# The feed-forward's first two steps begun on half the images, its steps then taken in threes

## The reference, cut to what matters

```python
x = x + conv_attention(group_norm(x))          # 4 heads of 32
t = tokens(x)                                   # 4 images x 256 tokens x 64
t = t + causal_attention(layer_norm(t))         # 4 heads of 16
xf = layer_norm(t)
gate_logits = xf @ Wg + bg                      # 8 logits a token
top_w, top_i = top_k(gate_logits, 2)
top_w = softmax(top_w)
w_dense = sum(one_hot(top_i, 8) * top_w[..., None], axis=1)
out = 0
for e in range(8):
    h = gelu(xf @ W1[e] + b1[e])                # 64 -> 256, exact gelu
    out = out + w_dense[:, e:e+1] * (h @ W2[e] + b2[e])   # 256 -> 64
t = t + out
```

## Time and profile before

| | us |
|---|---|
| median of 3 runs | 114.43 |
| the profiled execution | 114.85 |
| its span | 112.8 |
| PE busy in the span | 101.8 (90%) |
| DVE busy | 75.4 (67%) |
| ACT busy | 65.1 (58%) |
| granted clock of PE, mean | 0.998 of full |

### The profile page before, as it was taken

The page is one execution under the profiler, slowest core; times in us unless marked ns, Lnnn a source line. Parts: engine busy times, 40 slices in busy tenths (PEclk is TensorE's granted clock), DMA queues, the critical chain, the costliest instruction groups (busy, mean ns, idle before and its releaser), DMA issues.

```text
span 112.8 us, 2251 instructions
## 1 busy us (share of the span) xinstructions
PE 101.8 (90%) x831; PEld 52.8 (47%) x831; DVE 75.4 (67%) x210; ACT 65.1 (58%) x121; POOL 15.8 (14%) x28
## 2 busy tenths in 40 slices
PE   5989978889899999997899998999999999999920
PEld 2346456655555455566666654675342323232300
DVE  6965899979505469999966688998638453155250
ACT  4039973433888756564329958894937644764400
POOL 7900200000000000000000000000003941343140
PEclk9999999999999999999999999999999999999999
DMA  2940000199700000000000000000000000000003
GB/s 74 246 84 7 2 0 9 31 237 189 118 0 0 0 9 0 0 0 0 6 0 6 0 0 0 0 0 3 0 6 0 0 0 0 0 0 0 0 0 93
DMA packets 6633, 3.16 MB, mean 28 GB/s; under 512 B 4432, under 2 KB 6496, under 8 KB 6624
## 3 DMA queue, kind: packets, MB, share of 16 engines
q1 hardware_dynamic: 5936, 2.38, 11.5%
q10 hardware_dynamic: 688, 0.66, 2.3%
HBM read 2.77 MB, written 0.26 MB: 27 GB/s over the span
## 4 chain that ended last, share of the span: by engine, by line
PE 68%; DVE 16%; ACT 10%; issue 3%; DVEq 0%; ACTq 0%
PE bank L933 13%; PE bank L944 13%; PE bank L874 6%; PE bank L807 6%; PE bank L839 5%; PE bank L888 4%; PE bank L858 4%; PE bank L749 3%; PE bank L758 3%; PE bank L721 2%; DVE mx L590 2%; DVE mx L586 2%; ACT sq L399 2%; PE bank L845 1%; ACT sq L405 1%
## 5 line engine op out<-in xcount | busy, mean ns | idle before, releaser
L481 ACT ACTIVATE hid<-bank,b1c 128x1024 f32<-128x1024 f32 x16 | 16.9, 1112 | 11.8 <-PE bank L933 11.8
L437 ACT ACTIVATE pr<-bank 128x1024 f32<-128x1024 f32 (+1 forms) x16 | 14.0, 914 | 8.5 <-PE bank L845 5.1
L933 PE MATMUL bank<-xn,w_sb 64*128 64x512 f32 x64 | 15.6, 612 | 0.0
L944 PE MATMUL bank<-hid,w_sb 128*64 128x512 f32 x64 | 15.3, 603 | 0.0
L705 DVE SCALAR_TENSOR_TENSOR yw<-bank,b2c,wc 128x512 f32<-128x512 f32 x8 | 6.0, 748 | 12.6 <-PE bank L944 12.6
L721 PE MATMUL bank<-still 128*128 128x512 bf16 (+1 forms) x41 | 11.8, 437 | 1.2 <-DVE still L495 1.2
L359 POOL TENSOR_TENSOR acc<-yw,x 64x512 f32<-64x512 f32 x1 | 1.3, 1269 | 72.1 <-DVE yw L705 72.1
L586 DVE TENSOR_REDUCE mx<-bank 128x4 f32<-128x1024 f32 x8 | 9.3, 1218 | 0.9 <-PE bank L807 0.8
L807 PE MATMUL bank<-k,q 32*128 32x256 f32 (+1 forms) x128 | 8.3, 373 | 1.6 <-ACT q L425 0.6
L933 PEld LDWEIGHTS bank<-xn,w_sb 64*128 64x128 f32 x64 | 5.6, 186 | 8.5 <-ACT hid L481 4.4
L364 POOL TENSOR_TENSOR acc<-acc,yw 128x512 f32<-128x512 f32 x6 | 7.6, 1274 | 11.8 <-DVE yw L705 11.6
(11 more groups left out here) (148 smaller groups left out, 176.4 us busy)
## 6 DMA issues: line engine op xcount, KB each, us to landing
w_sb<-in_L_ffn_W_dram SPq DMA_DIRECT2D x3, 512.0 KB, 7.2
x<-in_x_dram ACTq DMA_DIRECT2D x2, 256.0 KB, 4.8
xg<-in_x_dram SPq DMA_DIRECT2D x1, 256.0 KB, 3.2
wg<-in_L_conv_w_qkv_dram SPq DMA_DIRECT2D x2, 96.0 KB, 4.8
bqkv<-in_L_attn_b_qkv_dram SPq DMA_DIRECT2D x12, 0.1 KB, 1.6
wo1t<-in_L_attn_W_out_dram SPq DMA_DIRECT2D x8, 4.0 KB, 1.8
out_dram<-acc SPq DMA_DIRECT2D x1, 128.0 KB, 2.5
out_dram<-acc ACTq DMA_DIRECT2D x1, 128.0 KB, 2.8
```

The lines of the kernel that those rows point to most:

```text
L437: nc.scalar.activation(pr[:, b, 2 * p:2 * p + 2, 0:n], two(key, 0, n), ACT.Exp, scale=SCALE[l]).then_inc(free(key), 1)
L481: nc.scalar.activation(hid[:, k % 4, :, :], two(("h", 0, k)), ACT.Gelu, bias=b1c[:, k:k + 1]).then_inc(free(("h", 0, k)), 1)
L933: i = mm(ps(key, i=s), w1_sb[r, e, P * j:P * j + P], XN[r, 2 * s:2 * s + 2, :].rearrange("p b t -> p (b t)"), start=True, stop=True)
L944: i = mm(ps(key, p0=C * s, p1=C * s + C), w2_sb[:, k, :], hid[:, k % 4, s, :], start=(j == 0), stop=(j == FT - 1))
```

## The change

The first two steps of the feed-forward are split by images. The halves of images 0 and 1 (`uphalf`) stand on PE behind the gate of image 1, ahead of the fillers and the gate of image 2. The halves of images 2 and 3 (`uprest`) stand behind the gate of image 2, ahead of the gate of image 3, which thereby moves behind them. The fillers ahead of the gate of image 3 (4 of 512 columns) go, and 4 of 256 columns stand ahead of `uprest` instead. So that the halves are contiguous per bank, the lower partitions now take images 0 and 2, the upper ones images 1 and 3; the gate tiles, the residual add of POOL and the two stores follow this.

The feed-forward then goes by threes: three ups, three downs. `hid` has 6 buffers for 4. The first such group is up 2, 3, 4, the transposes of the gate weights, up 5, and then downs 0, 1, 2. The bank pairs are 0/1, 4/5, 2/3.

```diff
-    ("gate", 2, (218, 222, 230, 234), ((7,), (2,), (7,), (2,))),
-    ("logits", 2, (221, 231, 233, 235), ()),
+    ("gate", 2, (218, 222, 232, 238), ((7,), (2,), (7,), (7,))),
+    ("logits", 2, (221, 233, 235, 239), ()),
+    ("uphalf", 2, (223, 224), ((0,), (4,))),
+    ("uprest", 2, (236, 237), ()),
...
-        hid = sb("hid", [P, 4, 2, HALF])
+        hid = sb("hid", [P, 6, 2, HALF])
...
-                    nc.gpsimd.tensor_tensor(acc[0:C, :], yw[0:C, 0, :], X[0:C, 0:2, :].rearrange("p b t -> p (b t)"), ALU.add).then_inc(summed, 1)
+                    nc.gpsimd.tensor_tensor(acc[0:C, :].rearrange("p (b t) -> p b t", b=2), yw[0:C, 0, :].rearrange("p (b t) -> p b t", b=2),
+                                            X[0:C, 0:3:2, :], ALU.add).then_inc(summed, 1)
...
             def gate(l, b):
                 key = ("logits", l, b)
                 claim(pe, key)
-                idle(key, (2, 2, 4, 4)[b])
+                idle(key, (2, 2, 4, 0)[b])
...
+            def up_part(k, n):
+
+                key = ("h", 0, k)
+                if n == 0:
+                    claim(pe, key)
+                elif k == 0:
+                    idle(key, 4, T)
+                pe.wait_ge(ld["w1"], 32)
+                pe.wait_ge(S["xn", 2], 2 * n + 2)
+                e, j = divmod(k, FT)
+                for s in range(2):
+                    r = slice(C * s, C * s + C)
+                    i = mm(ps(key, T * n, T * n + T, i=s), w1_sb[r, e, P * j:P * j + P], XN[r, 2 * n + s, :],
+                           start=(n == 0), stop=True, skip_group_check=True)
+                if n:
+                    i.then_inc(full(key), 1)
+
+            def up(k):
+
+                key = ("h", 0, k)
+                claim(pe, key)
+                e, j = divmod(k, FT)
+                for s in range(2):
+                    r = slice(C * s, C * s + C)
+                    i = mm(ps(key, i=s).rearrange("p (b t) -> p b t", b=2), w1_sb[r, e, P * j:P * j + P], XN[r, s:s + 3:2, :],
+                           start=True, stop=True)
+                i.then_inc(full(key), 1)
...
-            up(0)
-            up(1)
-            pe.wait_ge(ld["w2"], 16)
-            for e in range(E):
-                if e + 1 < E:
-                    up(FT * e + 2)
-                    up(FT * e + 3)
-                down(FT * e)
-                down(FT * e + 1)
-                if e == 0:
-                    key = ("gate_t", 0)
...
+            up(2)
+            for first in range(0, NK, 3):
+                for k in range(first + 3, min(first + 6, NK)):
+                    if k == 5:
+                        gate_turn()
+                    up(k)
+                if first == 0:
+                    pe.wait_ge(ld["w2"], 16)
+                for k in range(first, min(first + 3, NK)):
+                    down(k)
```

More of the change, by code:

```diff
@@ L71 @@
     ("var", 2, (194, 199, 214, 219), ()),
[L72 to L76, removed]
-    ("gate", 2, (218, 222, 230, 234), ((7,), (2,), (7,), (2,))),
-    ("logits", 2, (221, 231, 233, 235), ()),
+    ("ln", 2, (198, 201, 216, 227), ()),
+    ("r", 2, (200, 205, 220, 229), ()),
+    ("r2", 2, (208, 213, 225, 230), ()),
+    ("xr", 2, (204, 209, 226, 231), ()),
+    ("xn", 2, (212, 217, 228, 234), ()),
+    ("gate", 2, (218, 222, 232, 238), ((7,), (2,), (7,), (7,))),
+    ("logits", 2, (221, 233, 235, 239), ()),
+    ("uphalf", 2, (223, 224), ((0,), (4,))),
+    ("uprest", 2, (236, 237), ()),
 )
@@ L102, in hybrid_block @@
     ORDER = [(step, l, b, banks[b] if banks else ()) for _, step, l, b, banks in
-             sorted((place[b], step, l, b, banks) for step, l, place, banks in PLAN for b in range(B))]
+             sorted((at, step, l, b, banks) for step, l, place, banks in PLAN for b, at in enumerate(place))]
     seat, nth, follows = {}, {}, {}
@@ L138, in hybrid_block @@
             take(("logits", l, b), banks[0])
-    for k in range(NK):
-        take(("h", 0, k), 2 * (k % 3), 2)
-    take(("gate_t", 0), 7)
+        elif step == "uphalf":
+            take(("h", 0, b), banks[0], 2)
+    take(("h", 0, 2), 2, 2)
+    for k in range(3, NK):
+        take(("h", 0, k), seat["h", 0, k % 3], 2)
+    last_pair = 12 - sum(seat["h", 0, k] for k in range(3))
+    take(("gate_t", 0), last_pair + 1)
     for e in range(E):
-        take(("y", 0, e), 6 + e % 2)
+        take(("y", 0, e), last_pair + e % 2)
     with ExitStack() as ctx:
@@ L317, in _ @@
             sp.wait_ge(result, 1)
-            sp.dma_start(oo[:, 0:2, :], acc[0:C, :].rearrange("p (b t) -> p b t", b=2)).then_inc(stored, 16)
+            sp.dma_start(oo[:, 0:3:2, :], acc[0:C, :].rearrange("p (b t) -> p b t", b=2)).then_inc(stored, 16)
             sp.wait_ge(stored, 32)
@@ L358, in _ @@
                 if e == 0:
[L359 removed]
+                    nc.gpsimd.tensor_tensor(acc[0:C, :].rearrange("p (b t) -> p b t", b=2), yw[0:C, 0, :].rearrange("p (b t) -> p b t", b=2),
+                                            X[0:C, 0:3:2, :], ALU.add).then_inc(summed, 1)
                     pool.wait_ge(summed, 1)
[L361 removed]
+                    nc.gpsimd.tensor_tensor(acc[C:P, :].rearrange("p (b t) -> p b t", b=2), yw[C:P, 0, :].rearrange("p (b t) -> p b t", b=2),
+                                            X[C:P, 1:4:2, :], ALU.add).then_inc(summed, 1)
                 elif e < E - 1:
@@ L474, in gelus @@
                 filled(act, ("h", 0, k))
-                if k >= 4:
-                    e, j = divmod(k - 4, FT)
+                if k >= 6:
+                    e, j = divmod(k - 6, FT)
                     if j == FT - 1:
@@ L480, in gelus @@
                         act.wait_ge(hused, e + 1)
-                nc.scalar.activation(hid[:, k % 4, :, :], two(("h", 0, k)), ACT.Gelu,
+                nc.scalar.activation(hid[:, k % 6, :, :], two(("h", 0, k)), ACT.Gelu,
                                      bias=b1c[:, k:k + 1]).then_inc(free(("h", 0, k)), 1)
@@ L489, in _ @@
             act.wait_ge(result, 1)
-            act.dma_start(oo[:, 2:4, :], acc[C:P, :].rearrange("p (b t) -> p b t", b=2)).then_inc(stored, 16)
+            act.dma_start(oo[:, 1:4:2, :], acc[C:P, :].rearrange("p (b t) -> p b t", b=2)).then_inc(stored, 16)
             act.wait_ge(stored, 32)
@@ L629, in logits @@
                 key = ("logits", l, b)
-                tiles = slice(KT * b, KT * b + KT)
+                first = TH * (b % 2) + KT * (b // 2)
+                tiles = slice(first, first + KT)
                 filled(dve, key)
@@ L635, in logits @@
                 emptied(dve, key)
-                for t in range(KT * b, KT * b + KT):
+                for t in range(first, first + KT):
                     i = nc.vector.max(m8[:, t, :], lg[:, t, :])
@@ L919, in _ @@
                     gate(l, b)
+                elif step == "uphalf":
+                    up_part(b, 0)
+                elif step == "uprest":
+                    up_part(b, 1)
                 if (step, l, b) == ('var', 0, 2):
                     prep_rest()
[L923 to L935, removed]
             def down(k):
@@ L943, in down, with gate_turn @@
                 for s in range(2):
-                    i = mm(ps(key, p0=C * s, p1=C * s + C), w2_sb[:, k, :], hid[:, k % 4, s, :],
+                    i = mm(ps(key, p0=C * s, p1=C * s + C), w2_sb[:, k, :], hid[:, k % 6, s, :],
                            start=(j == 0), stop=(j == FT - 1))
                 i.then_inc(*((full(key), 1) if j == FT - 1 else (hused, 1)))
-            up(0)
-            up(1)
-            pe.wait_ge(ld["w2"], 16)
-            for e in range(E):
-                if e + 1 < E:
-                    up(FT * e + 2)
-                    up(FT * e + 3)
-                down(FT * e)
-                down(FT * e + 1)
-                if e == 0:
-                    key = ("gate_t", 0)
[L960 to L964, removed]
+            def gate_turn():
+                key = ("gate_t", 0)
+                claim(pe, key)
+                pe.wait_ge(gsteps, 7)
+                for j in range(TH):
+                    i = nc.tensor.transpose(ps(key, P * j, P * j + P), wd[:, j, :, :].rearrange("p q c -> p (q c)"), ident[:, :])
+                i.then_inc(full(key), 1)
+            up(2)
[8 more added lines that the diff above has]
+                    down(k)
 _INS = ['x', 'L0_conv_g', 'L0_conv_w_qkv', 'L0_conv_w_out', 'L0_conv_b_out', 'L1_attn_W_qkv', 'L1_attn_b_qkv',
```

## The result

The changed kernel took 115.88 us (median of 4 runs, 115.46 to 117.49) for 114.49 of the kernel before beside it: ratio 1.0109, 95% interval 1.007 to 1.0148. Measured again (first experiment), 115.89 for 114.74, ratio 1.0101, 1.0079 to 1.0122. By the ratios it is slower by 1.15 to 1.25 us where 0.57 was forecast, and 115.88 lies above the range's 115.50. The ratios leave out executions in a slower state, here the one of 117.49; with it the medians lie 1.39 apart.

What follows compares the result with a forecast made beforehand. PE's work between the second gate and the last downs was taken to bound the kernel. Fillers -0.43, boundaries gone -0.56, new boundaries +0.71 and stop +0.85 sum to +0.57 us: 115.00 on the median of 114.43, range +0.25 to +0.9.

Steps and rivals of the forecast that it cites:

- The way of PE: PE's start times from second gate to last downs, followed step by step; the end moves from 107.96 to 108.53, +0.57 us.
- Fillers: Ahead of the last gate on PE, four of 512 columns become four of 256: -0.43 us.
- boundaries: Changes of PE's array form: three between ups and downs go, -0.56 us; four new ones come, +0.71 us.
- halves at whole pace: Splitting ups 0 and 1 by images costs PE nothing beyond a boundary; each group of halves takes 1.06 us.
- Rival A: New boundaries on PE are free, other terms hold: -0.14 us, 114.29; chance 0.10.
- rival C: Halves go at the pace of their weight loads, 0.32 a pass: +1.23 us, 115.66; chance 0.09 shared with D.
- rival B: No stop ahead of the transposes, DVE's chain behind the gate taking under 2.8 us: -0.28, 114.15; chance 0.07.
- D: PE's longer stop brings a lower clock behind it, landing above rival C; chance 0.09 shared with rival C.
- The stop: PE waits ahead of the transposes for `wd`, 3.62 us behind the ups' start against 2.77 of work: +0.85 us.
- may stand 0.1 late: Up 4, due at 81.2, waits for gelu 1 behind tanh on ACT until 81.3, hidden in the stop.
- a gelu is named ahead of an up: Sign of a wrong forecast: an up on PE waiting for ACT; no size given.
- The time around the span: Time outside first to last instruction, kept at 2.05 us: profiled execution 114.85 becomes 115.42, span 112.8 becomes 113.4.

Runs made afterwards that it cites:

- first experiment: The changed kernel as it is, measured once more against the kernel before: 115.89 us, ratio 1.0101.
- threes_bank2: Changed kernel with ups 0 and 1 whole behind the last gate, fillers 2, 2, 4, 4, last gate in bank 2 as before: 114.54 us, ratio 0.9974.
- halves_only: Changed kernel keeping the halves, their fillers and the new layout, but with the old pairs of ups and downs behind them: 114.96 us, ratio 1.0018.
- turn_late: Changed kernel with the transposes of the gate weights behind up 5 instead of ahead of it: 114.80 us, ratio 1.0005.
- stop_in_old: Kernel before with the transposes placed behind up 2, nothing else changed: 116.54 us, ratio 1.0163.
- stop_filled: Changed kernel with four fillers of 512 columns ahead of the transposes, in the place of PE's stop: 115.56 us, ratio 1.0075.
- late_halves: Changed kernel with the last gate, in bank 2, ahead of the second halves, and fewer fillers: 114.65 us, ratio 0.9989.
- pad_late_halves: late_halves with the 13 starting fillers of 512 columns made into 11 of 512 and 11 of 128: 114.63 us, ratio 0.9998.
- threes_only: Changed kernel with ups 0 and 1 whole, fillers 2, 2, 4, 4, and the last gate left in bank 7: 115.25 us, ratio 1.0051.

## Why the prediction was right, and where it was wrong

**The way of PE: right.** Second gate to transposes was forecast step by step, and the starts came as follows: halves 74.91 for 74.91, fillers 75.98 for 75.97, third gate 76.85, fillers of 256 77.22 for 77.21, second halves 77.74 for 77.73, last gate 78.81 for 78.79, ups 79.35 for 79.33, transposes 82.97 for 82.95, end of the last downs 108.56 for 108.53. Fillers, boundaries and halves at whole pace stand (by threes_bank2, halves_only and the starts above). Rival A (free boundaries) and rival C (halves at the pace of weight loads) are refuted by the 1.06 of each group of halves, rival B by the DVE pieces in the chain. For D there is no sign: the granted clock was 1.00 in every stretch from 60 to 108.5 us. That the measured 115.88 lies nearest to C's 115.66 is chance; C's cause isn't there.

**The stop: right in size, half right in cause.** It is 0.85 (79.35 to 82.97 less 2.77). The text said that up 4 "may stand 0.1 late"; it began 0.24 late and lost 0.34 in the changed kernel, and ups 4 and 5 together lost 0.49 in turn_late. So a gelu is named ahead of an up, one of the prediction's own signs of being wrong, and the stop's size came out only because `wd` was later still. A wait in the middle of a group costs 0.10 more than it lasts in these rows, even the wait of 0.04 at up 5 in turn_late; why isn't shown.

**The time around the span: wrong.** The step that failed is the last sentence of the sum, "The profiled execution of 114.85 (span 112.8 and 2.05 around it) would become 115.42". I took the 2.05 as a constant of the measurement, and so put its change at 0. It isn't constant: when both kernels were measured again, the median around the span was 2.51 in the changed kernel and 1.80 in before. That growth of 0.7 covers the 0.6 to 0.7 by which the difference in time missed. What the runs show in its place is that PE's stop ahead of the transposes brings it (stop_in_old has it, turn_late and stop_filled don't), and that it comes with a fetch of a 16 KB instruction block behind the span. The Trainium skill, "Runtime: NRT & Kernel Launch", Instruction fetch mechanics, says that instructions are refilled in 16 KiB blocks, that crossing a border is mostly hidden, and that a taken branch to a target outside the window forces a fetch before execution goes on. The trace agrees with the block's size, and with hidden fetches inside the span (PE stays busy for the whole stretch 99 to 100 in stop_filled); no run here shows what a taken branch does. That the program's end waits for the late block is an inference from the 16 traces and the times, as what runs behind the span isn't in the trace: the block could also be a companion of a late end with another cause.

**What stays open.** What puts the fetch behind the span. It came with the stop ahead of the transposes in five kernels, also in the old order, and went when fillers stood in the stop; but it came in late_halves and pad_late_halves too, without such a stop, and not in threes_only, which waited 0.70 elsewhere. The number of PE's instructions doesn't decide it alone: the changed kernel and turn_late have the same number, and a different outcome.

## What to carry to other kernels

A step that is moved late on the busy engine moves the start of every chain on other engines that hangs on it: count the work left between it and the first instruction that needs the chain's end, and do it for each queue that the chain passes, since a small operation in ACT's queue (tanh) holds back the gelus behind it. When a wait is removed, say what lies just under it. And compare the span and the time separately: a term that the trace doesn't hold can be as large as the effect.

## What the runs showed of the hardware that was not expected

Around the span lie 1.8 to 1.9, 2.1 or 2.5 to 2.8 us in the median, by kernel, with a late 16 KB instruction fetch in each trace of the last kind; leaving 8 PE instructions out took 0.63 us of it in one kernel and nothing in two others. Halved ups, of 64 rows and 256 columns, lose nothing by the halving (1.06 us for a group, where the same columns in whole ups with one boundary take 0.853 + 0.21), and reading two images 512 elements apart instead of side by side costs nothing (ups in threes: 2.78, three times the old slope and one boundary).
